# The similarity projection from a row-scaled triangle of M: 64 products for each pair instead of 72, in another order of lists

## The chip, the core and the metric

The kernel runs on one core of a Trainium2 chip. The metric is the device time of one launch in microseconds (us); lower is better.

## The reference, cut to what matters

```python
z_l = h @ W_lang.T ; z_g = h @ W_grav.T ; v = h @ W_V.T      # h: 32 graphs of 256 nodes x 512 features
A_l = max(cosine(z_l, z_l), 0) * not_eye                      # 256 x 256
A_g = exp(-|z_g[n] - z_g[m]|^2 / (2 sigma^2)) * not_eye
K   = w_l * rows_to_one(A_l * adj) + (1 - w_l) * rows_to_one(A_g * adj)
x   = layernorm(x + (K @ v) @ W_O.T)
```

All tensors are float32.

## The kernel before, in words

For each of the two metrics g (L for W_lang, G for W_grav) the kernel forms the symmetric 512 x 512 matrix M = W^T W once. It needs z z^T = h M h^T only in symmetric form, so it computes one matrix X = h^T-side times P, with P = (a part of M) h, and takes X + X^T. Every float32 operand of TensorE is split in two rounded parts (hi and lo, type fp32r): h in `hT_hi`, `hT_lo`; M in `m_hi`, `m_lo`, the halved diagonal blocks in `md_hi`.

**Preparation** (lines 1273 to 1310 on TensorE, `prep_units` at line 282). Units of TensorE work in a fixed list: UPPER (one block row of M's upper triangle), MIRROR (its transposes for the lower blocks), WO_TURN, WVO (the value weights). Four banks of PSUM are used in turn, so a unit waits for the rest part of the fourth unit before it (`prep_lo`, line 1278). ScalarE writes the hi part (line 627; line 628 the halved diagonal block), VectorE the rest (lines 874, 876) and the MIRROR copies (line 869). GpSimd meanwhile splits W_V (lines 516 and 518) and clears the diagonal of the adjacency matrix (lines 524, 527).

**Pairs of graphs.** The 32 graphs are worked through in 16 pairs. TensorE's list of a pair p (line 1413) has, in this order: eight projections (`project`, banks in turn, each waiting until VectorE has finished the one four before it, `proj_ready`, line 1318), the value product 0, four tiles of X (`x_tile`; the first waits for all eight projections, line 1347), value product 1, K times V of graph 0 of the pair before (`k_times_v`), value products 2 and 3, K times V of graph 1. It is a program of 176 matmuls of 512 columns, 72 of them projections:

```python
for i in range(DT):
    steps.append((m_hi[:, g, i, c], lo[i]))
    if i <= j:
        steps.append((m_hi[:, g, i, c] if i < j else md_hi[:, g, i], hi[i]))
        steps.append((m_lo[:, g, i, c], hi[i]))
```

so that the projections of feature block j = 0, 1, 2, 3 have 6, 8, 10 and 12 products, for both g in turn.

Each engine has its own written list of a pair. ScalarE (line 721) rounds each projection (`proj_hi_part`, line 662), saves X, subtracts its diagonal (`centre`), takes exp, scales, rounds K and does the layer norm. VectorE (line 1055) makes the rest parts (`proj_lo_part`, line 921), reads diagonals (line 932), turns blocks (lines 844, 957, 1034), masks and sums, combines K (line 1025), makes its rest part (line 1041) and adds the residual (line 1051). GpSimd (line 572) computes powers of short vectors. SP's list (line 434) holds all transfers of a pair, X and K being spilled to HBM and read back turned. One pair's chain from X to K times V is spread over two passes of these lists: q = p - 1 is the pair before. Passes 0 and 1 and the last two are written out, the rest is a loop of two pairs. The last pair has lists of its own (lines 787, 1189, 1437), which the change leaves as they are.

Of the kernel before, what the change touches and what calls it, by code (L numbers as in the profile page):

```python
# [31 lines left out]
EPS = 1e-8  # L32
LN_EPS = 1e-5
P = 128
# [3 lines left out]
def gnn_resnorm(nc, x, adj, w_lang, w_grav, w_v, w_o, gate_logit, log_sigma, out):  # L38
# [14 lines left out]
    with ExitStack() as ctx:  # L53
# [52 lines left out]
        rden = sb("rden", [P, 2, 2, NT])  # L106
# [15 lines left out]
        scal = sb("scal", [P, 8])  # L122
        last_coef = sb("last_coef", [P, 2, 2, NT])
        last_mean = sb("last_mean", [P, 2, NT])
        last_rstd = sb("last_rstd", [P, 2, NT])
        last_shift = sb("last_shift", [P, 2, NT])

# [85 lines left out]
        adj_ready = sem("adj_ready")  # L213
        scal_exp = sem("scal_exp")
# [82 lines left out]
        def prepared(kind, g, i):  # L297

            return prep_units.index((kind, g, i)) + 1

# [53 lines left out]
        def _(sp):  # L354
# [79 lines left out]
            def pair(p):  # L434

                q = p - 1
                return_x(q, 1)
                spread_r(q, 1)
                load_blocks(p + 1, 1)
                load_x(q, 0)  # L440
                load_x(q, 1)
                spill_k(q, 0)
                load_blocks(p + 2, 0)
                return_k(q, 0)
                spill_k(q, 1)
                store(q - 1, 0)
                store(q - 1, 1)
                spill_x(p, 0)
                store_r(p, 0)
                return_k(q, 1)  # L450
                spread_r(p, 0)
                return_x(p, 0)
                spill_x(p, 1)
                store_r(p, 1)
# [45 lines left out]
        def _(pool):  # L500
# [8 lines left out]

            for k in range(DT):  # L510
                pool.wait_ge(w_loaded[L][k], 16)
# [9 lines left out]

            pool.wait_ge(adj_loaded, 16)
            for t in range(NT):
# [4 lines left out]
                                  r_row[:].rearrange("p t (k a) -> p k t a", a=BLK)).then_inc(adj_ready, 1)  # L528

# [73 lines left out]
        def _(act):  # L603
# [15 lines left out]
            def prep_hi_part(u):  # L619
# [29 lines left out]
            def proj_hi_part(p, k):  # L649
# [6 lines left out]
                if k < 2 * DT:  # L656
                    dst = p_hi[:, :, k // 2, k % 2, :]
                    src = src[:].rearrange("p (b n) -> p b n", b=2)
                else:
                    b, t = divmod(k - 2 * DT, NT)  # L660
                    dst, src = last_v(m_hi, b, t) if is_last(p) else v_hi[:, b, t], src[:]
                nc.scalar.copy(dst, src).then_inc(proj_hi, 1)  # L662
# [58 lines left out]
            def pair(p, parity):  # L721

                q = p - 1
                proj_hi_part(p, 0)
                proj_hi_part(p, 1)
                squares(q - 1, 0)
                proj_hi_part(p, 2)
                proj_hi_part(p, 3)
                proj_hi_part(p, 4)
                gauss_scaled(q, 0)  # L730
                squares(q - 1, 1)
# [4 lines left out]
                normalise(q - 1, 0)  # L736
                gauss_scaled(q, 1)
                save_x(p, 0, 0)
                save_x(p, 0, 1)
                normalise(q - 1, 1)  # L740
                centre(p, 0)
                kt_hi_part(q, 0)
                save_x(p, 1, 0)
                save_x(p, 1, 1)
                turn_hi(p + 1, 1 - parity, 1)
                proj_hi_part(p, 8)
                proj_hi_part(p, 9)
                centre(p, 1)
                kt_hi_part(q, 1)
                proj_hi_part(p, 10)  # L750
                proj_hi_part(p, 11)
                turn_hi(p + 2, parity, 0)
                gauss(p, 0)

            turn_hi(1, 1, 0)
            pair(0, 0)
# [79 lines left out]
        def _(dve):  # L836
# [25 lines left out]
            def prep_lo_part(u):  # L862
# [9 lines left out]
                if kind == UPPER:  # L872
                    if e < D:
                        nc.vector.tensor_tensor(m_lo[:, g, i, e:], src[:, e:], m_hi[:, g, i, e:].bitcast(F32),
                                                ALU.subtract)
                    nc.vector.scalar_tensor_tensor(out=m_lo[:, g, i, a:e], in0=src[:, a:e], scalar=0.5,
# [10 lines left out]
            for u in range(PREP):  # L887
# [4 lines left out]
                if u in SPLIT_AT:  # L892
                    turn_lo(0, 0, SPLIT_AT[u])
# [591 lines left out]
```

## Time and profile before

| | us |
|---|---|
| median of 3 runs (lowest to highest) | 686.14 (685.93 to 686.62) |
| the profiled execution, its own time | 686.16 |
| its span, first to last instruction | 684.4 |
| busy: TensorE, VectorE, ScalarE, GpSimd | 675.4, 518.0, 364.7, 132.4 |

The profile is of one execution. Busy times overlap between engines; a span on GpSimd is rough, and a matmul's drawn duration is longer than its distance to the next, since matmuls are pipelined. What counts on TensorE is the distance between starts. PEld is the load of the stationary operand, which runs beside the matmuls. "Idle before, releaser" tells what an engine waited for.

### The profile page before, as it was taken

The page shows a single profiled execution, that of the slowest core. Times are in us where ns is not written, and L with a number is a line of the kernel's source. Part 1 is how long each engine was busy: PE and PEld are TensorE (multiplying, and loading weights), DVE is VectorE, ACT ScalarE, POOL GpSimd, SP SyncE. Part 2 cuts the span into 40 slices and gives each one's busy share as a digit, 9 for nine tenths or more (in the row PEclk, how much of TensorE's full clock was granted, in tenths as well). Part 3 has the DMA queues.
Part 4 walks back from the last instruction along what each step waited for, and adds up shares of the span by engine and source line. Part 5 has one row for each costly group of instructions (what it writes and reads, how often), then busy time and mean ns, then how long its engine had stood idle before and what let it go on. Part 6 is the DMA issues. An engine that isn't in the chain of part 4 may idle for free.

```text
span 684.4 us, 10995 instructions
## 1 busy us (share of the span) xinstructions
PE 675.4 (99%) x3020; PEld 559.6 (82%) x3020; DVE 518.0 (76%) x1396; ACT 364.7 (53%) x705; POOL 132.4 (19%) x278
## 2 busy tenths in 40 slices
PE   8999999999999999999999999999999999999995
PEld 7888888888888888888888888888888888888884
DVE  4645878788697878869787886978788697877876
ACT  5434445645455564545556454555645455564646
POOL 3302021111222111122211112221111222121122
PEclk9999999999999999999999999999999999999999
DMA  9312726473664647366464636646473664636523
GB/s 291 92 34 67 218 79 191 127 209 112 194 184 141 189 132 197 115 197 181 140 188 131 202 112 196 182 140 188 136 196 112 194 184 141 186 109 184 162 70 123
DMA packets 141510, 106.50 MB, mean 156 GB/s; under 512 B 40112, under 2 KB 115632, under 8 KB 141488
## 3 DMA queue, kind: packets, MB, share of 16 engines
q1 hardware_dynamic: 140768, 104.40, 51.2%
q0 software_dynamic: 288, 1.05, 0.5%
q10 hardware_dynamic: 432, 0.79, 0.3%
q8 instruction: 10, 0.16, 0.1%
q14 instruction: 12, 0.10, 0.0%
HBM read 65.80 MB, written 40.40 MB: 155 GB/s over the span
## 4 chain that ended last, share of the span: by engine, by line
PE 98%; DMA 0%; DVE 0%; issue 0%; ACT 0%; POOL 0%; POOLq 0%
PE bank L1264 95%; PE bank L1286 2%; DMA xs<-in_L_gnn_W_lang 0%; PE bank L1368 0%; PE bank L1296 0%; PE bank L1291 0%; PE bank L1378 0%; DVE xq L1166 0%; DVE p_lo L858 0%; ACT p_hi L617 0%; POOL last_rstd L589 0%; POOLq L53 0%; DVE xq L1186 0%; DVE last_shift L1181 0%; DVE last_rstd L1175 0%
## 5 line engine op out<-in xcount | busy, mean ns | idle before, releaser
L1264 PE MATMUL bank<-hT_lo,m_hi 128*128 128x512 f32 x512 | 168.0, 389 | 0.0
L662 ACT CAST p_hi<-bank 128x512 fp32r<-128x512 f32 x128 | 73.5, 588 | 101.4 <-PE bank L1264 101.4
L1264 PE MATMUL bank<-hT_hi,m_lo 128*128 128x512 f32 x320 | 124.5, 389 | 0.0
L921 DVE TENSOR_TENSOR p_lo<-bank,p_hi 128x512 fp32r<-128x512 f32 x128 | 85.3, 687 | 39.1 <-ACT p_hi L662 37.5
L1264 PEld LDWEIGHTS bank<-hT_lo,m_hi 128*128 128x128 f32 x512 | 96.1, 188 | 20.1 <-DVE p_lo L921 0.2
L662 ACT CAST v_hi<-bank 128x512 fp32r<-128x512 f32 x60 | 32.5, 590 | 132.1 <-PE bank L1264 132.1
L1264 PE MATMUL bank<-wvo_hi,hT_hi 128*128 128x512 f32 x256 | 99.8, 390 | 0.0
L1264 PE MATMUL bank<-wvo_hi,hT_lo 128*128 128x512 f32 x256 | 99.6, 389 | 0.0
L1264 PE MATMUL bank<-wvo_lo,hT_hi 128*128 128x512 f32 x256 | 99.6, 389 | 0.0
L1264 PE MATMUL bank<-p_lo,hT_hi 128*128 128x512 f32 x256 | 99.6, 389 | 0.0
L1264 PE MATMUL bank<-p_hi,hT_hi 128*128 128x512 f32 x256 | 99.6, 389 | 0.0
L537 POOL TENSOR_TENSOR rnorm<-norm,minus_half 128x2 f32<-128x2 f32 x32 | 35.3, 1103 | 256.0 <-DVE norm L938 256.0
L1264 PE MATMUL bank<-hT_hi,m_hi 128*128 128x512 f32 x192 | 74.7, 389 | 0.0
L1264 PEld LDWEIGHTS bank<-hT_hi,m_lo 128*128 128x128 f32 x320 | 60.1, 188 | 12.6
L1051 DVE SCALAR_TENSOR_TENSOR y<-bank,x_nat 128x512 f32<-128x512 f32 x60 | 39.7, 678 | 36.1 <-PE bank L1264 36.1
L932 DVE CUSTOM_DVE_ANT_0 junk_d<-xs,ident 128x128 f32<-128x128 f32 x128 | 29.6, 287 | 38.6 <-ACT xs L673 38.6
L673 ACT COPY xs<-bank 128x512 f32<-128x512 f32 x64 | 36.1, 585 | 38.0 <-PE bank L1264 37.9
L1264 PEld LDWEIGHTS bank<-wvo_hi,hT_hi 128*128 128x128 f32 x256 | 48.1, 188 | 10.0
L1264 PEld LDWEIGHTS bank<-p_hi,hT_hi 128*128 128x128 f32 x256 | 48.1, 188 | 10.0
L1264 PEld LDWEIGHTS bank<-wvo_lo,hT_hi 128*128 128x128 f32 x256 | 48.1, 188 | 9.9
L1264 PEld LDWEIGHTS bank<-p_lo,hT_hi 128*128 128x128 f32 x256 | 48.0, 188 | 10.0
L1264 PEld LDWEIGHTS bank<-wvo_hi,hT_lo 128*128 128x128 f32 x256 | 48.0, 187 | 10.0
(140 smaller groups left out, 1213.4 us busy)
## 6 DMA issues: line engine op xcount, KB each, us to landing
x_blk<-in_x SPq DMA_DIRECT2D x128, 128.0 KB, 3.0
x_spill<-xs SPq DMA_DIRECT2D x30, 512.0 KB, 3.4
xq<-x_spill SPq DMA_DIRECT2D x120, 128.0 KB, 3.1
x_nat<-in_x SPq DMA_DIRECT2D x30, 512.0 KB, 4.7
out_y<-y SPq DMA_DIRECT2D x30, 512.0 KB, 3.0
k_spill<-work SPq DMA_DIRECT2D x30, 256.0 KB, 2.1
work<-k_spill SPq DMA_DIRECT2D x120, 64.0 KB, 2.1
r_row<-r_spill SPq DMA_DIRECT2D x32, 128.0 KB, 3.5
```

The source lines that it names most:

```text
L537: nc.gpsimd.tensor_tensor(rnorm[:, b, 0:NT], norm2[:, b], minus_half[:], ALU.pow).then_inc(pool_steps, 1)
L662: nc.scalar.copy(dst, src).then_inc(proj_hi, 1)
L673: nc.scalar.copy(dst, src).then_inc(x_saved, 1)
L921: nc.vector.tensor_tensor(dst, src, hi.bitcast(F32), ALU.subtract).then_inc(proj_ready, 1)
L932: ins = nc.vector.tensor_tensor_reduce(out=junk_d[:, g, t].rearrange("p (j a) -> p j a", a=BLK), in0=block, in1=ident[:].rearrange("p (j a ...
L1051: nc.vector.scalar_tensor_tensor(out=y[:, b, t], in0=kv_bank[t][:], scalar=1.0, in1=x_nat[:, b, t], op0=ALU.mult, op1=ALU.add, accum_out=r ...
L1264: last = pe.matmul(dst, lhsT, rhs, start=(n == 0), stop=(n == len(steps) - 1))
L1286: last = pe.matmul(dst[:, cols], lhsT, rhs, start=(n == 0), stop=(n == len(steps) - 1))
```

## The change

For a symmetric M any matrix T with T + T^T = M serves on the hi part of h. Before, T was the upper triangle, in hi and rest parts. Now T has, below the diagonal, the hi entries of M alone, and above it the rests; the row of T that belongs to output feature d is scaled by s(d), a number close to 1 with which the rounded diagonal entry becomes exact, and the rests (`m_lo`) are corrected for it. Each block of T is then one rounded operand: `m_lo` for i < j, the joined block `md_hi` for i = j, `m_hi` for i > j. With the four products of `hT_lo` that makes 8 products for every projection, 64 in all.

What else it touches: the scale s is applied where the projection leaves PSUM (ScalarE by an activation with a scale of one number per partition, VectorE by a scalar_tensor_tensor); the four L projections come first, then the four G (`of_projection`); the first projection of a pair waits for the hi parts of h alone and for the rests after four products. In the preparation VectorE reads the diagonals (`diagonals`), computes s (`scales`) and corrects the rests (`scaled_rest`), GpSimd makes two masks and joins the diagonal blocks (`join_triangles`), ScalarE no longer writes a halved block and VectorE has one rest operation for a unit instead of two. The lists of a pair on VectorE, ScalarE and SP are written in another order; `rden` is dropped for `den`.

```diff
@@ GpSimd
+            def join_triangles(g):
+                pool.wait_ge(m_scaled[g], DT)
...
+                for part, (tile, mask) in enumerate(((m_hi, lower_half), (m_lo, upper_strict))):
+                    many, one = diagonal_blocks(tile, g)
+                    nc.gpsimd.tensor_tensor(triangle(part)[:, 0:DT - 1], many.bitcast(F32),
+                                            mask.unsqueeze(1).broadcast_to([P, DT - 1, P]), ALU.mult).then_inc(m_parts[g], 1)
+                    nc.gpsimd.tensor_tensor(triangle(part)[:, DT - 1], one.bitcast(F32), mask, ALU.mult).then_inc(m_parts[g], 1)
+                pool.wait_ge(m_parts[g], 4)
+                nc.gpsimd.tensor_tensor(md_hi[:, g], triangle(0), triangle(1), ALU.add).then_inc(m_ready[g], 1)
@@ ScalarE
-                    nc.scalar.copy(m_hi[:, g, i, i * P:], src[:, i * P:])
-                    nc.scalar.mul(md_hi[:, g, i], src[:, i * P:(i + 1) * P], 0.5).then_inc(prep_hi, 1)
+                    nc.scalar.copy(m_hi[:, g, i, i * P:], src[:, i * P:]).then_inc(prep_hi, 1)
...
+                    nc.scalar.activation(p_hi[:, :, j, g, :], src[:].rearrange("p (b n) -> p b n", b=2), ACT.Copy,
+                                         scale=m_scale[:, g, j:j + 1]).then_inc(proj_hi, 1)
@@ VectorE, preparation
+            def diagonals(g, i):
+                dve.wait_ge(prep_lo, prepared(UPPER, g, i))
+                for s, (tile, sign) in enumerate(((m_hi, 1.0), (m_lo, -1.0))):
+                    nc.vector.tensor_tensor_reduce(
+                        out=x_nat[:, g, s, a:e], in0=tile[:, g, i, a:e].bitcast(F32), in1=ident[:], scale=sign, scalar=0.0,
+                        op0=ALU.mult, op1=ALU.add, accum_out=steps_of[g][:, s, i:i + 1]).then_inc(m_scale_steps[g], 1)
+            def scaled_rest(g):
+                for i in range(DT):
+                    nc.vector.scalar_tensor_tensor(
+                        out=m_lo[:, g, i, i * P:], in0=m_hi[:, g, i, i * P:].bitcast(F32), scalar=steps_of[g][:, 4, i:i + 1],
+                        in1=m_lo[:, g, i, i * P:].bitcast(F32), op0=ALU.mult, op1=ALU.add).then_inc(m_scaled[g], 1)
...
+                if kind == UPPER and g == L:
+                    diagonals(L, i)
+                    if i == DT - 1:
+                        scales(L)
+                        scaled_rest(L)
+                if kind == UPPER and g == G and i < DT - 1:
+                    diagonals(G, i)
...
+                if (kind, g, i) == (MIRROR, G, 1):
+                    diagonals(G, DT - 1)
+                    scales(G)
+                if (kind, g, i) == (WVO, None, 1):
+                    scaled_rest(G)
@@ VectorE, a pair: the order now (lo k is proj_lo_part)
+ gram(q,0,L) gauss_masked(q,0) lo0 cosine_masked(q,0) row_factors(q,0) lo1 lo2 turn_x(q,1) lo3
+ kernel_sum(q,0) gram(q,1,G) lo4 inverse_masked(q,1) gram(q,1,L) lo5 lo6 lo7 gauss_masked(q,1)
+ cosine_masked(q,1) row_factors(q,1) turn_lo(p+1,0) kernel_sum(q,1) diagonal(p,0) turn_k(q,0)
+ turn(p+1,1) turn_r(p,0) kt_lo(q,0) diagonal(p,1) turn_lo(p+1,1) residual(q,0,0) turn(p+2,0) lo8
+ turn_r(p,1) turn_k(q,1) lo9 kt_lo(q,1) residual(q,0,1) turn_x(p,0) gram(p,0,G) residual(q,1,0)
+ residual(q,1,1) lo10 inverse_masked(p,0) lo11
@@ SP, a pair: the order now
+ load_blocks(p+1,1) load_blocks(p+2,0) return_x(q,1) spread_r(q,1) spill_k(q,0) return_k(q,0)
+ store(q-1,0) spill_k(q,1) load_x(q,0) spill_x(p,0) return_k(q,1) store_r(p,0) return_x(p,0)
+ spill_x(p,1) store(q-1,1) load_x(q,1) spread_r(p,0) store_r(p,1)
@@ TensorE
                 for i in range(DT):
+                    stationary = m_lo[:, g, i, c] if i < j else md_hi[:, g, i] if i == j else m_hi[:, g, i, c]
+                    pe.matmul(pbank(k)[:], stationary, hi[i], start=(i == 0), stop=False)
+                if k == 0:
+                    pe.wait_ge(hT_ready, upto(p, 2, 2))
+                for i in range(DT):
+                    last = pe.matmul(pbank(k)[:], m_hi[:, g, i, c], lo[i], start=False, stop=(i == DT - 1))
```

In the first pair TensorE waits for `m_ready[L]` before projection 0 and for `m_ready[G]` before projection 4; VectorE waits for both before its first list.

## Rows read from the trace of the kernel before

**Rows 1.** The page, busy time of each engine and TensorE's granted clock in tenths

```profile
PE 675.4 (99%) x3020; PEld 559.6 (82%) x3020; DVE 518.0 (76%) x1396; ACT 364.7 (53%) x705; POOL 132.4 (19%) x278
...
PEclk9999999999999999999999999999999999999999
```

**Rows 2.** The chain that ended last: start us, us, what

```profile
30.39 624.78 PE bank L1264 x2756
```

**Rows 3.** One pair, its projections: us, then busy (x) of PE, PEld, DVE, ACT, POOL

```profile
349.40:389.30 39.90, 39.90 (x178) 33.03 (x176) 31.41 (x85) 21.86 (x42) 7.74 (x16) 1.00 0.53 165
349.40:365.70 16.30, 16.30 (x73) 13.51 (x72) 14.72 (x37) 9.96 (x21) 3.61 (x9) 1.00 0.61 176
```

**Rows 4.** Groups: out<-in, shapes xcount | busy us, mean ns | idle before

```profile
L1264 PE MATMUL bank<-hT_lo,m_hi 128*128 128x512 f32 x512 | 168.0, 389 | 0.0
...
L1264 PE MATMUL bank<-hT_hi,m_lo 128*128 128x512 f32 x320 | 124.5, 389 | 0.0
...
L1264 PE MATMUL bank<-hT_hi,m_hi 128*128 128x512 f32 x192 | 74.7, 389 | 0.0
```

**Rows 5.** Groups: emptying a projection, and the nearest rows to its new forms

```profile
L662 ACT CAST p_hi<-bank 128x512 fp32r<-128x512 f32 x128 | 73.5, 588 | 101.4 <-PE bank L1264 101.4
...
L921 DVE TENSOR_TENSOR p_lo<-bank,p_hi 128x512 fp32r<-128x512 f32 x128 | 85.3, 687 | 39.1 <-ACT p_hi L662 37.5
...
L1051 DVE SCALAR_TENSOR_TENSOR y<-bank,x_nat 128x512 f32<-128x512 f32 x60 | 39.7, 678 | 36.1 <-PE bank L1264 36.1
...
L685 ACT ACTIVATE work<-work,scal 128x512 f32<-128x512 f32 x25 | 18.2, 730 | 0.0
```

**Rows 6.** Timeline of that pair: start us, us, what, idle before and its releaser

```profile
348.24 0.69 DVE L1051 SCALAR_TENSOR_TENSOR y<-bank,x_nat 128x512 f32<-128x512 f32 x1 [2.49 <-PE bank L1264]
...
376.39 0.65 DVE L1041 TENSOR_TENSOR kt_lo<-work,kt_hi 128x512 fp32r<-128x512 f32 x1
...
378.42 0.39 PE L1264 MATMUL bank<-v_hi,kt_hi 128*128 128x512 f32 x1
```

**Rows 7.** Transfers by line: KB each, median us from issue to landing

```profile
xq<-x_spill SPq DMA_DIRECT2D x120, 128.0 KB, 3.1
x_nat<-in_x SPq DMA_DIRECT2D x30, 512.0 KB, 4.7
```

**Rows 8.** Timeline of the last pair: TensorE and VectorE

```profile
628.66 0.39 PE L1264 MATMUL bank<-hT_lo,m_hi 128*128 128x512 f32 x1
...
631.87 0.68 DVE L921 TENSOR_TENSOR p_lo<-bank,p_hi 128x512 fp32r<-128x512 f32 x1
...
646.61 0.69 DVE L921 TENSOR_TENSOR p_lo<-bank,p_hi 128x512 fp32r<-128x512 f32 x1
...
647.75 0.39 PE L1264 MATMUL bank<-p_hi,hT_hi 128*128 128x512 f32 x1
```

**Rows 9.** Timeline of the preparation: GpSimd, VectorE, TensorE

```profile
14.12 0.61 POOL L516 CAST v_hi<-xq 128x512 fp32r<-128x512 f32 x1 [6.24 <-DMA xq<-in_L_gnn_W_V]
14.81 1.29 POOL L518 TENSOR_TENSOR v_lo<-xq,v_hi 128x512 fp32r<-128x512 f32 x1
...
17.28 0.56 DVE L874 TENSOR_TENSOR m_lo<-bank,m_hi 128x384 fp32r<-128x384 f32 x1 [2.85 <-ACT md_hi L628]
...
18.92 0.38 PE L1291 MATMUL bank<-ident,m_hi 128*128 128x128 f32 x2
...
35.70 0.39 PE L1264 MATMUL bank<-hT_lo,m_hi 128*128 128x512 f32 x1
```

**Rows 10.** GpSimd and VectorE side by side in one pair, and a group

```profile
334.32 0.69 POOL L537 TENSOR_TENSOR rnorm<-norm,minus_half 128x2 f32<-128x2 f32 x1 [11.03 <-DVE norm L938]
...
338.04 1.23 DVE L852 TENSOR_TENSOR hT_lo<-hT_raw,hT_hi 128x1024 fp32r<-128x1024 f32 x1
338.27 1.54 POOL L537 TENSOR_TENSOR rnorm<-norm,minus_half 128x2 f32<-128x2 f32 x1 [2.34 <-DVE norm L938]
...
L932 DVE CUSTOM_DVE_ANT_0 junk_d<-xs,ident 128x128 f32<-128x128 f32 x128 | 29.6, 287 | 38.6 <-ACT xs L673 38.6
```

More of the change, by code:

```diff
@@ L32 @@
 EPS = 1e-8
+TINY = 1e-35
 LN_EPS = 1e-5
@@ L122, in gnn_resnorm @@
         scal = sb("scal", [P, 8])
+        m_scale = sb("m_scale", [P, 2, DT])
         last_coef = sb("last_coef", [P, 2, 2, NT])
@@ L126, in gnn_resnorm, with diagonal_blocks, split_blocks, triangle @@
         last_shift = sb("last_shift", [P, 2, NT])
+        lower_half = junk_d[:, 0, 0]
+        upper_strict = junk_d[:, 0, 1]
+        steps_of = [junk_d[:, 1, 1, 32 * g:32 * g + 32].rearrange("p (s j) -> p s j", j=DT) for g in range(2)]
+        def diagonal_blocks(tile, g):
+            flat = tile[:, g].rearrange("p k d -> p (k d)")
+            step = D + P
+            return (flat[:, 0:(DT - 1) * step].rearrange("p (i w) -> p i w", w=step)[:, :, 0:P], flat[:, (DT - 1) * step:])
+        def split_blocks(tile, g):
+            flat = tile[:, g].rearrange("p k c -> p (k c)")
+            return (flat[:, 0:(DT - 1) * P].rearrange("p (i c) -> p i c", c=P), flat[:, (DT - 1) * P:])
+        def triangle(part):
+            return junk_a[:].rearrange("p t (k c) -> p t k c", c=P)[:, part]
         COS, GAUSS, KER = range(3)
@@ L213, in gnn_resnorm @@
         adj_ready = sem("adj_ready")
+        masks_cleared = sem("masks_cleared")
+        masks_ready = sem("masks_ready")
+        m_scale_steps = [sem(f"m_scale_steps{g}") for g in range(2)]
+        m_scaled = [sem(f"m_scaled{g}") for g in range(2)]
+        m_parts = [sem(f"m_parts{g}") for g in range(2)]
+        m_ready = [sem(f"m_ready{g}") for g in range(2)]
         scal_exp = sem("scal_exp")
@@ L299, in prepared, with of_projection @@
             return prep_units.index((kind, g, i)) + 1
+        def of_projection(k):
+            return k % DT, k // DT
         def upto_unit(u):
@@ L1081, in pair @@
                 turn_k(q, 0)
+                turn(p + 1, 1)
                 turn_r(p, 0)
-                turn(p + 1, 1)
                 kt_lo_part(q, 0)
@@ L1086, in pair @@
                 turn_lo(p + 1, 1 - parity, 1)
+                residual(q, 0, 0)
+                turn(p + 2, 0)
+                proj_lo_part(p, 8)
                 turn_r(p, 1)
-                turn(p + 2, 0)
-                residual(q, 0, 0)
-                residual(q, 0, 1)
-                proj_lo_part(p, 8)
                 turn_k(q, 1)
@@ L1312, in project @@
             def project(p, parity, k):
-                j, g = divmod(k, 2)
+                j, g = of_projection(k)
                 if k == 0:
-                    pe.wait_ge(hT_ready, upto(p, 2, 2))
+                    pe.wait_ge(hT_hi_ready, upto(p, 2, 2))
+                if type(p) is int and p == 0 and j == 0:
+                    pe.wait_ge(m_ready[g], 1)
+                    pe.wait_ge(prep_lo, prepared(MIRROR, g, DT - 1))
                 if not (type(p) is int and p == 0 and k < 4):
```

129 lines of the change are left out of this document (76 added, 53 removed).

## The prediction, made blind

> **What bounds the kernel now.** The page comes first: TensorE is busy for 675.4 of 684.4 us at the full granted clock, 2.4 GHz, and no other engine is over 76% [rows 1]. Busy time alone doesn't make a bound, so the chain of waits is next: one unbroken piece of 624.78 us holds 2,756 products of line 1264 [rows 2], 0.2267 us from start to start. A pair is 176 of them, 39.9 us, which is what the stage table shows for one pair, with VectorE busy for 31.4 us and ScalarE for 21.9 [rows 3]. So every product taken out of a pair gives back 0.2267 us, as long as the other engines' lists keep up. They have less room than their averages tell: within the projections VectorE is busy for 14.7 of 16.3 us [rows 3].
>
> **Products removed.** The projections are 72 a pair: 512, 320 and 192 in the three groups [rows 4], and 128 with the halved diagonal blocks, 1,152 over 16 pairs. Afterwards 64 x 16 = 1,024. 128 x 0.2267 = **-29.0 us**. A pair becomes 168 x 0.2267 = 38.1 us.
>
> **Emptying a projection.** VectorE's subtraction, 687 ns, becomes a scalar_tensor_tensor from PSUM; the residual, 678 ns, has that form [rows 5]. I take no change. ScalarE's cast, 588 ns, becomes an activation with a scale for each partition. Bounds: 0 to +0.14 us, by the 730 ns of the nearest activation over 512 columns [rows 5]; I take the upper end, 1.1 us a pair on an engine with 16 us to spare, and 0.14 us later for VectorE.
>
> **The order within a pair.** I laid the new lists beside TensorE's, from T, the start of a pair: projection k ends at 1.81(k+1), the value product at 17.2, the X tiles at 19.1 to 24.5, K times V of graph 0 runs from 27.2 and that of graph 1 from 35.4 to 38.1. A result reaches ScalarE 0.2 us later. Durations are those of before (a rest part 0.60 us from start to start). VectorE's pass ends with the residual that the last product releases, then lo10, the masked inverse and lo11: free at T+2.7. After the L sum and the masked exp it makes lo0 by T+4.6; projection 4 wants it at T+7.3. With the cosine, the factors and the turn between, lo3 is ready at T+9.0 (wanted at 12.7), lo4 at T+11.6 behind ScalarE's scaling and layer norm (wanted at 14.5), lo7 at T+16.1 (wanted by the first X tile at 17.2). X must be saved at T+21.7 for the fourth tile at 22.7. K's rest part of graph 0 is ready at T+25.7 for 27.2, a margin of 1.5 us; before, it ended at 377.04 for 378.42, 1.4 us [rows 6]. On SP the load of x for graph 1, once issued early in a pair, now stands behind the second store: issued at T+32.3, landing 4.7 us later at T+37.0 [rows 7], just when the residual of graph 1 wants it at 36.9; some tenths there are covered, since VectorE waited 2.49 us for TensorE ahead of that residual [rows 6]. The return of X of graph 1 goes behind eight block loads (3.7 us of issues): issued by T'+2.4 of the next pair, landing 3.1 us later [rows 7] at T'+5.5, wanted at T'+7.1. Every margin is at least 1.0 us, so the steady pairs cost **0**. If VectorE's cover of lo7 (1.1 us) were gone, each 0.1 us beyond it would cost 1.4 us over the 14 pairs.
>
> **The last pair** keeps its lists, made for projections of 6 to 12 products. There VectorE works without a pause from lo0 at 631.87 to lo7, ended at 647.30, 18.64 us after the first projection at 628.66; the X tile wanted it at 647.75 [rows 8], 19.09 after. The wish moves to 17.2. The chain starts 0.4 us sooner, so lo7 comes at 18.2: **+1.0 us** (between 0.5 and 2).
>
> **The preparation.** Removed: eight halved blocks on ScalarE (0.17 us each) and eight small rest operations on VectorE (some 0.15 us each, merged). Added on VectorE for each g: eight diagonal readings of 0.22 us from start to start (287 ns each [rows 10]), four tiny steps of 0.2, four corrections of 0.6, 0.47, 0.34 and 0.2: 4.2 us. For L they fit mostly into VectorE's idle time of 2.85 us before the rest part at 17.28 [rows 9]: without anything else the cost is 0.4 us, where the rests of WO_TURN come 0.3 us late. For G, the joins on GpSimd are 384, 128, 384, 128 and 512 columns at the 1.29 us for 512 of its two-input row [rows 9]: 4.1 us. The correction of G ends near 36.2, the join at 40.4; projection 4 of the first pair wants it at 35.70 [rows 9] + 7.3 = 43.0. Covered, with 2.6 us to spare, and VectorE's wait for it covered too.
>
> But the L part falls into the time in which GpSimd works without a gap on W_V, 14.12 to 21.8 [rows 9]. The trace shows that the two engines get in each other's way: a GpSimd operation of 0.69 us took 1.54 when it met VectorE's two-input subtraction that had begun at 338.04, and ended 0.54 us after it [rows 10]. The other direction no row shows. Bounds: 0.4 us if VectorE never waits. If it waits for a GpSimd operation at each of its instructions with two SBUF inputs, two diagonal readings, one small step and the four corrections alternate with the eight operations on W_V; the correction ends at 22.3, not 17.3, the rest of the first G unit at 22.9, and TensorE's MIRROR at 18.92 starts at 23.0: 4.1 us late. The G diagonals against the L join then add up to 4: 8 in all. I take **+5 us**, all of the L part and one more, since the row shows the handover within such meetings, and the G part has idle time before it. The Trainium skill (SBUF — State Buffer, "Who interferes with whom") states both directions: a VectorE instruction with two SBUF inputs and a GpSimd one that reads SBUF exclude each other for a whole instruction. By that rule the term is nearer its upper end; the trace agrees as far as rows 10 go.
>
> Sum: 686.16 - 29.0 + 1.0 + 5.0 = 663.2 us; the profiled execution is 0.02 us above the median.
>
> **Rivals.**
> (a) VectorE does not wait for GpSimd: the preparation costs 0.4 us, 658.6 us. For it: no row shows the wait. Against it: the opposite wait is plain [rows 10].
> (b) A steady wait: one of the margins of 1.0 to 1.6 us is gone, say by 0.3 to 0.8 us in each pair, because lo7, X's copy or K's rest part is later than my tally; 14 x 0.3 to 0.8 = 4 to 11 us on top of either case, 665 to 675. For it: VectorE's list is nearly full in the projections [rows 3]. Against: its busy time in a pair is 31.4 of 38.1 us, and nothing big is added.
> (c) Slower than before: SP, which works strictly in order, becomes the pace. Its return of X of graph 0 now follows the return of K and the store of norms; from there the chain goes over the turned X, exp and the masked exp to lo0, with 4.7 us of slack at the masked exp and 2.7 at lo0. If it came over 7.4 us late in each pair, each pair would wait, and from 7.4 + 1.8 us the gain would be gone; at 10 us late, 686.2 - 29.0 + 16 x 2.6 = 699 us. For it: the waits for centred X, for K and for the layer norm now stand in one row ahead of it. Against: its issues are 22 us of 38.
> That the change doesn't do what it says is excluded by its loops: eight products a projection are written out.
>
> **The numbers.** Forecast 0.5; (a) 0.3; (b) 0.17; (c) 0.03. Predicted 663.2 us. The range reaches down to (a) with all 29.0 us kept, 657.5, and up to 8 us of preparation and a little of (b), 669. About 0.2% can be told from no change here. Faster 0.96, within it 0.01, slower 0.03.
>
> **What the profile would show.** 64 projection products a pair and 168 x 0.2267 = 38.1 us from one pair's start to the next; no waits of TensorE in the loop (b would show them ahead of an X tile or of K times V); a gap of about 1 us before the first X tile of the last pair; in the preparation diagonal readings and corrections on VectorE stretched or late beside the splits of W_V, a MIRROR that starts near 23 and the first projection near 41 instead of 35.7. Were this at 36, (a) holds; a pair longer than 38.3 us would make the forecast wrong in its main part.

## The result, and the profile after

| | before | after |
|---|---|---|
| median of 4 runs each, us (lowest to highest) | 686.03 (685.80 to 686.62) | 666.14 (664.92 to 666.75) |
| profiled execution, its span | 686.16, 684.4 | 666.75, 665.0 |
| mean granted clock of TensorE in it | 0.998 | 0.993 |

The ratio of the runs is 0.9706, 95% interval 0.969 to 0.9723: 19.9 us faster. The forecast of 663.2 us was 2.9 us too low, inside its range of 657.5 to 669.0. The span shrank by 19.4 us, where the sum of the prediction had 23.0.

The page of the changed kernel: busy time of each engine, the granted clock, and the groups that answer to [rows 1, 4, 5]. In it and below, line 1435 has the products of a projection with `hT_hi`, 1439 those with `hT_lo`, 1370 the other products of the pairs, X tiles among them, and those of WVO, 1397 the MIRROR transposes, 718 ScalarE's and 1016 VectorE's part of emptying a projection; where an experiment adds or removes lines, these numbers shift by up to three.

```profile
PE 650.5 (98%) x2892; PEld 538.4 (81%) x2892; DVE 538.7 (81%) x1438; ACT 376.6 (57%) x697; POOL 138.8 (21%) x292
...
PEclk9799999999999999999999999999999999999999
...
L1439 PE MATMUL bank<-hT_lo,m_hi 128*128 128x512 f32 x512 | 136.8, 389 | 0.0
L718 ACT ACTIVATE p_hi<-bank,m_scale 128x512 fp32r<-128x512 f32 x128 | 87.6, 686 | 74.3 <-PE bank L1439 73.3
...
L1016 DVE SCALAR_TENSOR_TENSOR p_lo<-bank,m_scale,p_hi 128x512 fp32r<-128x512 f32 x128 | 92.7, 742 | 17.8 <-ACT p_hi L718 17.5
```

3,020 matmuls have become 2,892: the 128 are gone. ScalarE's scaled cast takes 686 ns where the plain one took 588; VectorE's scaled rest takes 742 where the subtraction took 687. The second digit of the clock row is a 7 where before there were only nines.

The chain of waits of the changed kernel, two neighbouring pairs, and the stage table of one pair (columns as in [rows 3]):

```profile
91.08 23.57 PE bank L1370 x104
...
129.16 23.57 PE bank L1370 x104
```

```profile
349.40:387.48 38.08, 38.08 (x170) 31.53 (x169) 31.47 (x85) 22.67 (x42) 7.38 (x16) 1.00 0.61 171
```

A pair's 104 other products start 38.08 us after those of the pair before, 168 x 0.2267, and TensorE has no idle time in between. The first projection of the last pair starts at 609.53, that of the first pair at 43.77: 565.76 us for 15 pairs, where before it was 628.66 - 35.70 = 592.96. The difference, 27.20 us, is 15 x 8 x 0.2267. So the steady part is as forecast, to 0.01 us; what is left is ahead of it and behind it.

**Ahead: the preparation.** The timeline of the changed kernel, VectorE, GpSimd and TensorE (compare [rows 9]; line 947 reads a diagonal, 957 is the first tiny step of the scales, 968 corrects the rests, 560 is the second operation of a split of W_V):

```profile
14.81 1.06 DVE L947 CUSTOM_DVE_ANT_0 x_nat<-m_hi,ident 128x128 f32<-128x128 f32 x1
...
16.41 1.28 POOL L560 TENSOR_TENSOR v_lo<-xq,v_hi 128x512 fp32r<-128x512 f32 x1
16.52 1.20 DVE L957 TENSOR_SCALAR junk_d<-junk_d 128x4 f32<-128x4 f32 x1
...
18.38 4.33 DVE L968 SCALAR_TENSOR_TENSOR m_lo<-m_hi,junk_d,m_lo 128x512 fp32r<-128x512 f32 x4
...
23.36 0.44 PE L1397 MATMUL bank<-ident,m_hi 128*128 128x128 f32 x2 [3.92 <-DVE m_lo L935]
...
42.47 1.93 DVE L968 SCALAR_TENSOR_TENSOR m_lo<-m_hi,junk_d,m_lo 128x512 fp32r<-128x512 f32 x4
```

A diagonal reading takes 0.29 us alone and 1.06 beside a split. A step on 4 elements, begun 0.11 us after the split at 16.41, ends at 17.72, 0.03 us after the split does. The four corrections take 4.33 us beside the splits and 1.93 at 42.47, where GpSimd is idle. MIRROR, at 18.92 before, starts at 23.36: 4.44 us late. The same stretch as a table of stages (span, then busy of PE, PEld, DVE, ACT, POOL, then the granted clock):

```profile
22.00:24.00 2.00, 0.44 (x2) 0.20 (x2) 1.97 (x6) 0.00 (x0) 1.38 (x3) 0.96 0.00 0
24.00:26.00 2.00, 1.34 (x7) 1.35 (x8) 1.97 (x8) 0.19 (x1) 1.92 (x4) 0.50 0.04 8
26.00:28.00 2.00, 2.00 (x11) 2.00 (x11) 2.00 (x4) 0.39 (x1) 1.94 (x4) 0.50 0.01 4
28.00:30.00 2.00, 2.00 (x11) 2.00 (x11) 1.41 (x7) 0.51 (x2) 0.56 (x1) 0.50 0.00 0
30.00:32.00 2.00, 2.00 (x17) 1.98 (x15) 1.57 (x3) 1.03 (x2) 0.00 (x0) 0.83 0.00 0
```

After TensorE's idle 3.9 us its granted clock fell to 0.50, the 1.2 GHz level, some 0.2 us before the end of the first row, and stayed there until some 0.7 us into the last row (0.7 x 0.5 + 1.3 over 2 us gives the 0.83), some 6.8 us in all, although TensorE was busy again. The first projection came 8.07 us late: 4.44 for MIRROR, 0.9 for one more wait (the copy of line 931), and 2.7 that are left for the half clock. The preparation is the least steady part of the kernel: experiments 4, 5, 6, 7 and 11 leave it as it is, and in their traces the first projection starts at 43.81, 43.77, 43.18, 42.31 and 43.05. Over the six the delay is 6.6 to 8.1 us, and the traced execution lies at its upper end; a difference of up to 1.5 us between the first projections of two single traces can be there without any edit to the preparation.

**Behind: the last pair.** Its first projection and first X tile, and VectorE's first and last rest part between them, after:

```profile
609.53 0.39 PE L1435 MATMUL bank<-hT_hi,md_hi 128*128 128x512 f32 x1
...
612.40 0.74 DVE L1016 SCALAR_TENSOR_TENSOR p_lo<-bank,m_scale,p_hi 128x512 fp32r<-128x512 f32 x1
...
627.51 0.75 DVE L1016 SCALAR_TENSOR_TENSOR p_lo<-bank,m_scale,p_hi 128x512 fp32r<-128x512 f32 x1
...
628.32 0.50 PE L1370 MATMUL bank<-p_hi,hT_hi 128*128 128x512 f32 x1 [0.57 <-DVE p_lo L1016]
```

18.79 us from the first projection to the X tile, where 76 products need 17.23: 1.56 lost, and 0.30 less than the 19.09 before (84 products, 19.04, so that 0.05 was lost there). VectorE's chain from the start of lo0 to the end of lo7, without a pause in both kernels, takes 15.86 us; before it took 15.43 [rows 8]. From the X tile to the end it is 36.68 us (36.65 before). Together: -27.20 + 8.07 - 0.30 + 0.03 = -19.4 us, the whole difference of the spans.

### The profile page after: what moved, and what is told of

It is laid out like the page before. It is cut to its first block, busy times and chain, and to the rows that moved or that the text cites. A ratio compares the mean times of both kernels' runs of the same rounds, so it can differ in the third digit from the quotient of the medians.

```text
span 665.0 us, 10795 instructions
## 1 busy us (share of the span) xinstructions
PE 650.5 (98%) x2892; PEld 538.4 (81%) x2892; DVE 538.7 (81%) x1438; ACT 376.6 (57%) x697; POOL 138.8 (21%) x292
## 4 chain that ended last, share of the span: by engine, by line
PE 92%; DVE 4%; DMA 1%; ACT 1%; issue 0%; SPq 0%; POOL 0%; POOLq 0%; DVEq 0%; ACTq 0%
PE bank L1370 57%; PE bank L1435 16%; PE bank L1439 16%; PE bank L1392 1%; DMA x_nat<-in_x 1%; DVE m_lo L968 1%; DVE x_nat L947 1%; DMA xs<-in_L_gnn_W_lang 0%; PE bank L1402 0%; DVE p_lo L1016 0%; DVE work L1071 0%; PE bank L1478 0%; DVE m_lo L935 0%; DVE work L1105 0%; ACT y L778 0%
## 5 line engine op out<-in xcount | busy, mean ns | idle before, releaser
L1439 PE MATMUL bank<-hT_lo,m_hi 128*128 128x512 f32 x512 | 136.8, 389 | 0.0
L718 ACT ACTIVATE p_hi<-bank,m_scale 128x512 fp32r<-128x512 f32 x128 | 87.6, 686 | 74.3 <-PE bank L1439 73.3
L1016 DVE SCALAR_TENSOR_TENSOR p_lo<-bank,m_scale,p_hi 128x512 fp32r<-128x512 f32 x128 | 92.7, 742 | 17.8 <-ACT p_hi L718 17.5
L722 ACT CAST v_hi<-bank 128x512 fp32r<-128x512 f32 x60 | 34.9, 581 | 118.7 <-PE bank L1370 118.6
L1435 PE MATMUL bank<-hT_hi,m_lo 128*128 128x512 f32 x192 | 59.2, 390 | 0.3 <-DVE p_lo L1016 0.3
L1435 PE MATMUL bank<-hT_hi,m_hi 128*128 128x512 f32 x192 | 59.1, 389 | 0.0
L1435 PE MATMUL bank<-hT_hi,md_hi 128*128 128x512 f32 x128 | 49.8, 389 | 0.0
L623 POOL TENSOR_TENSOR msq<-row_sq,one_by_d 128x2 f32<-128x2 f32 x30 | 5.9, 198 | 197.8 <-ACT junk_a L770 197.7
```

The costliest lines, as they stand in the source:

```text
L718: nc.scalar.activation(p_hi[:, :, j, g, :], src[:].rearrange("p (b n) -> p b n", b=2), ACT.Copy, scale=m_scale[:, g, j:j + 1]).then_inc(pr ...
L722: nc.scalar.copy(last_v(m_hi, b, t) if is_last(p) else v_hi[:, b, t], src[:]).then_inc(proj_hi, 1)
L1016: nc.vector.scalar_tensor_tensor(out=p_lo[:, :, j, g, :], in0=src[:].rearrange("p (b n) -> p b n", b=2), scalar=m_scale[:, g, j:j + 1], in ...
L1435: pe.matmul(pbank(k)[:], stationary, hi[i], start=(i == 0), stop=False)
L1439: last = pe.matmul(pbank(k)[:], m_hi[:, g, i, c], lo[i], start=False, stop=(i == DT - 1))
```

## The experiments

The theory after the result: the steady pairs and the price of a product are as forecast; the 8 us are one cause and its follower, VectorE held by GpSimd's work on W_V, and TensorE's clock after the idle time that this makes. All runs change the changed kernel. "First projection" and "last pair" are the starts of the first projections of the first and the last pair in the profiled execution. The kernel before was timed again beside them: 686.75 us beside experiments 1, 2, 3 and 5, 685.98 beside 4, 6, 7 and 8, 685.86 beside 9, 10 and 11; each ratio is to that time. Where one execution is all there is (experiments 1, 3, 4, 5, 11), its time has no interval.

**1. GpSimd starts on W_V later.**

```diff
             for h in range(2):
                 load_w(pool, 2, w_v, h)
+            pool.wait_ge(m_scaled[L], DT)
             for k in range(DT):
```

> The changed kernel with one wait more: GpSimd starts to split W_V only when the L rests are corrected. VectorE's list is untouched. Theory (exclusion): VectorE's L part, ended at 22.6 us now, ends at 17.5 to 18, the wait at the MIRROR of block row 2 is gone; the splits end near 25.5, so the first WVO product waits for them, 1 to 3 us late; first projection at 37 to 40 us. Rival (VectorE's own work is the delay): the L part ends no sooner than 22 us and the first projection, with the splits delayed as well, starts later than 43.8.

One execution: 660.85 us, span 659.1, 5.9 under the changed kernel's. VectorE at the corrections, GpSimd at its first split, and VectorE's first step of the scales of G, in this run:

```profile
15.64 1.93 DVE L969 SCALAR_TENSOR_TENSOR m_lo<-m_hi,junk_d,m_lo 128x512 fp32r<-128x512 f32 x4
...
17.49 0.69 DVE L936 TENSOR_TENSOR m_lo<-bank,m_hi 128x512 fp32r<-128x512 f32 x1
...
17.65 0.61 POOL L559 CAST v_hi<-xq 128x512 fp32r<-128x512 f32 x1 [9.66 <-DVE m_lo L969]
...
28.68 1.20 DVE L958 TENSOR_SCALAR junk_d<-junk_d 128x4 f32<-128x4 f32 x1
```

The same instructions on the same data take 1.93 us, not 4.33, and all that has changed is that GpSimd is idle beside them. The wait of 3.9 us is gone, the clock was 1.00 in every stretch from 18 to 38, and the first projection came at 37.97 instead of 43.77. So an added wait makes the kernel faster; what VectorE does for L stayed in its place, so its own length is not what made these 5.8 us. The splits, now later, meet VectorE's work for G instead: a reading of G took 1.36 us beside a split, and the step on 4 elements shown last took 1.20 beside a join.

**2. VectorE's last reading, scales and corrections of L later**, behind the first rest part of WVO:

```diff
-                    diagonals(L, i)
-                    if i == DT - 1:
-                        scales(L)
-                        scaled_rest(L)
+                    if i < DT - 1:
+                        diagonals(L, i)
+                if (kind, g, i) == (WVO, None, 0):
+                    diagonals(L, DT - 1)
+                    scales(L)
+                    scaled_rest(L)
```

> The changed kernel, but VectorE reads the last L diagonal, computes the L scales and corrects the L rests only after the rest part of the first WVO unit, when GpSimd has long finished splitting W_V. Theory (the two engines exclude each other on operations that read SBUF, and TensorE then loses its clock too): no TensorE wait of 3.9 us at the MIRROR of block row 2, the four corrections take 1.9 us instead of 4.3, the first projection starts at 36 to 38 us instead of 43.8, and the time is 659 to 661 us. Rival (VectorE's added 4.2 us of work, wherever it stands, is what delays TensorE): the delay comes later in the preparation but stays, first projection at 41 us or later, 664 us or more.

663.0 us (662.59 to 663.42, two executions; ratio 0.9647, 0.9606 to 0.9688), 2 us above what I had written. First projection at 38.00, no idle 3.9 us and the clock at 0.999: the same answer from VectorE's side. But a part of the cost moved, as the waits of TensorE show:

```profile
PE bank L1437 <- DVE m_hi L931: 1.8, 1, 1.8
...
PE bank L1437 <- POOL md_hi L578: 0.8, 1, 0.8
```

The late corrections make the join of L late (0.8 us) and the copies of MIRROR that the first projections' banks wait for (1.8). The last pair starts 568.07 us after the first projection, not 565.76.

**3. TensorE kept busy through the wait.**

```diff
             for u in range(PREP):
+                if u == prepared(MIRROR, L, 2) - 1:
+                    for n in range(18):
+                        pe.matmul(kv_bank[1][:], kt_hi[:, 0, 0, 0], in_kt(kt_hi, 0), start=True, stop=True)
                 prepare(u)
```

> The changed kernel with 18 products of 512 columns of zeros into a free bank (about 4.1 us) ahead of the MIRROR unit that waits 3.9 us. Nothing else changes: VectorE's L part still ends at 22.6 us. Theory (of the 8.1 us by which the first projection starts later, 4.8 are waits and 3.3 the granted clock of 0.5 from 24 to 30.5 us that follows them): the clock stays at 1.0, TensorE still waits for VectorE until 23.4, the first projection starts at 40 to 41 us, the time falls by 3 us. Rival (all 8.1 us are waits for VectorE, the low clock covers nothing more): first projection at 43 us or later.

One execution: 664.92 us, span 663.2, no less than the lowest of the changed kernel's four, so the time alone shows nothing; the trace has to. Here the collision stays (the four corrections took 4.73 us) and only the fall of the clock is taken away; the stages of this run:

```profile
20.00:24.00 4.00, 3.37 (x16) 2.53 (x14) 3.96 (x6) 0.00 (x0) 3.92 (x4) 1.00 0.03 7
24.00:31.00 7.00, 5.63 (x43) 5.21 (x44) 6.93 (x21) 2.31 (x5) 4.86 (x8) 1.00 0.00 1
```

MIRROR started at 22.98 (23.36 in the changed kernel), the first projection at 41.90 (43.77). From MIRROR to the first projection it is 18.92 us, where the changed kernel has 20.41 and the five other traces with its preparation 19.9 to 21.1. So the half clock costs some 1.5 us that nothing else takes over (1.0 to 2.2 against the other traces); less than the 3 us I had expected, because at full clock TensorE next waits for VectorE (1.2 us at the MIRROR copies, 0.8 at `hT_lo`, in place of 0.9).

**4. L and G projections in turn again.**

```diff
-            return k % DT, k // DT
+            return k // 2, k % 2
```

> The changed kernel with L and G projections in turn as in the kernel before, instead of four L and then four G. The joined G block, ready at 48.7 us, is then wanted by the second projection at 45.6 instead of the fifth at 51.0. Theory: TensorE waits for it once, 2.5 to 3.5 us, in the first pair, and pairs stay at 38.08 us; 669 to 670 us. Rival (order within the projections does not matter, or matters in every pair since the G sums come first on VectorE): 666.8 us, or pairs over 38.2 us.

One execution: 669.94 us, as I had written, 3.2 us above the changed kernel's profiled run. TensorE, and what it waited for, in this run:

```profile
PE bank L1435 <- POOL md_hi L578: 2.9, 1, 2.9
```

GpSimd's join of G ended at 48.66. With L first, projection 4 needs it 7.3 us after projection 0; in turn, projection 1 does, after 1.8. This shows that the joins of G are covered in the changed kernel, and by what: there the join ended at 48.68 and projection 4 started at 51.03, 2.35 us to spare.

**5. The old order of the lists within a pair**, on VectorE, ScalarE and SP. The core of the edit on SP:

```diff
-                load_blocks(p + 1, 1)
-                load_blocks(p + 2, 0)
...
+                load_blocks(p + 1, 1)
+                load_x(q, 0)
+                load_x(q, 1)
...
-                store(q - 1, 1)
-                load_x(q, 1)
-                spread_r(p, 0)
```

> The changed kernel with the lists of a pair of VectorE, ScalarE and SP in the order of the kernel before; products, preparation and TensorE's list as changed. Theory (the old order was made for projections of 6 to 12 products; in it VectorE works through the q sums, masks and the turn ahead of lo6 and lo7, and the masked exp of graph 1 behind lo7): a pair gets longer than 38.1 us by 0.3 to 1.5 us, 671 to 687 us in all, with TensorE waiting for VectorE's p_lo ahead of the first X tile. Rival (the reordering gives nothing, the products alone give the gain): 38.1 us a pair, 665 to 668 us.

One execution: 667.47 us, span 665.5, within 0.5 of the changed kernel's. First projection 43.77, last pair 609.53, to the hundredth as with the new lists: the new order brings nothing to the steady pairs, and my theory that the old one would cost something in each pair was wrong. Only the last pair's X tile came 0.35 us later than in the changed kernel, 19.14 us after its first projection. The new order has one visible trace, a load that comes late. The line of the residual in the changed kernel, and in experiment 6:

**6. The load of x for graph 1 behind that of graph 0.**

```diff
                 load_x(q, 0)
+                load_x(q, 1)
                 spill_x(p, 0)
...
                 store(q - 1, 1)
-                load_x(q, 1)
```

> The changed kernel, but SP issues the load of x for graph 1 right behind that for graph 0 instead of behind the second store. Theory (the wait of VectorE's residual for that load, 1.6 to 1.7 us in each pair, is covered in the steady pairs but starts VectorE's unbroken chain in the last pair late): pairs stay at 38.08 us, the residual no longer waits for the load, the first X tile of the last pair comes 17.7 to 18.1 us after its first projection instead of 18.8, the time falls by 0.7 to 1.1 us. Rival (the last pair loses 1.5 us to its lists alone): no change, within 0.3 us.

```profile
609.37 0.69 DVE L1154 SCALAR_TENSOR_TENSOR y<-bank,x_nat 128x512 f32<-128x512 f32 x1 [1.74 <-DMA x_nat<-in_x]
```

```profile
607.78 0.69 DVE L1154 SCALAR_TENSOR_TENSOR y<-bank,x_nat 128x512 f32<-128x512 f32 x1 [0.73 <-PE bank L1370]
...
609.14 0.69 DVE L1154 SCALAR_TENSOR_TENSOR y<-bank,x_nat 128x512 f32<-128x512 f32 x1 [0.66 <-PE bank L1370]
```

The first fence is the changed kernel, the second this run: the wait for the transfer is gone. The time is 666.27 us (665.31 to 666.8; ratio 0.971, 0.9694 to 0.9727), the same as without the edit, so my theory was wrong and the rival right. In place of the one wait for the transfer VectorE now has two for TensorE, 0.73 and 0.66 us, and its lo0 starts 2.74 us after the last pair's first projection instead of 2.87. The X tile comes 18.67 us after it instead of 18.79, where I had expected 17.7 to 18.1.

**7. The last pair's list fitted to 8 products.** The rest parts of VectorE come sooner, the masked sums and the turn of K later, and ScalarE rounds projection 7 ahead of the first layer norm:

```diff
             proj_hi_part(p, 6)
+            proj_hi_part(p, 7)
             normalise(q - 1, 0)
-            proj_hi_part(p, 7)
...
-            cosine_masked(q, 1)
             proj_lo_part(p, 3)
+            cosine_masked(q, 1)
+            proj_lo_part(p, 4)
...
-            kernel_sum(q, 1)
             proj_lo_part(p, 5)
             proj_lo_part(p, 6)
-            turn_k(q, 0)
             proj_lo_part(p, 7)
+            kernel_sum(q, 1)
+            turn_k(q, 0)
```

> The changed kernel with the last pair's lists fitted to projections of 8 products: VectorE makes rest part 3 ahead of the cosine mask, 4 ahead of the exp mask, and 5 to 7 ahead of the sum of K of graph 1; ScalarE scales projection 7 ahead of the first layer norm. Theory (the last pair's 1.5 us are VectorE's queue ahead of the rest parts): the first X tile comes 17.3 to 18.0 us after the first projection instead of 18.8 and the end moves with it, 0.8 to 1.5 us less. Rival (the chain behind the X tiles, K of graph 1 by SP's spill and return, then sets the end): the X tile comes sooner and the time stays.

668.46 us (667.97 to 669.06; ratio 0.9746, 0.973 to 0.9763): 2.3 us slower. The rival that I had written down came true, and more than that, since it had the time stay. The X tile did come sooner, 18.18 us after the first projection instead of 18.79. But K of graph 1 was spilled later, and its return holds ScalarE's list, in this run:

```profile
633.64 0.71 DVE L1137 STREAM_TRANSPOSE work<-work 128x512 f32<-128x512 f32 x1 [3.78 <-DMA work<-k_spill]
...
634.44 0.62 ACT L761 CAST kt_hi<-work 128x512 fp32r<-128x512 f32 x1 [3.64 <-DVE work L1137]
...
636.77 0.66 PE L1478 MATMUL bank<-ident,xs 128*128 128x128 f32 x4 [2.53 <-ACT xs L739]
```

Behind that cast in ScalarE's order stands the centring of X, behind that turn in VectorE's order the reading of X's diagonal, and TensorE waited 2.53 us for the centred X. The lost 1.56 us in the last pair can't be had by this reordering; whether by another I did not try.

**8. The preparation spread on VectorE's side**: scales of L and two diagonals of G behind MIRROR of G, block row 1, corrections of L behind the first WVO rest part, the last diagonal and the scales of G behind the second, corrections of G behind the last MIRROR.

```diff
-                    if i == DT - 1:
-                        scales(L)
-                        scaled_rest(L)
...
+                if (kind, g, i) == (WVO, None, 0):
+                    scaled_rest(L)
...
                 if (kind, g, i) == (MIRROR, G, 1):
+                    scales(L)
+                    diagonals(G, 0)
+                    diagonals(G, 1)
+                if (kind, g, i) == (WVO, None, 1):
                     diagonals(G, DT - 1)
                     scales(G)
-                if (kind, g, i) == (WVO, None, 1):
+                if (kind, g, i) == (MIRROR, G, DT - 1):
                     scaled_rest(G)
```

> The changed kernel with the preparation's VectorE work spread over its idle times behind GpSimd's splits of W_V: L scales and the first two G diagonals after the first G MIRROR copy, the corrections of L after the first WVO rest part, the last G diagonal and the G scales after the second, the corrections of G after the last MIRROR copy. Only the fourth L diagonal still meets the splits. Theory (exclusion): no wait over 1 us of TensorE in the preparation, full clock throughout, first projection at 36 to 37 us, the join of G done by 42.5 us and not waited for; 658.5 to 660.5 us in all. Rival (VectorE's added work is the cost): first projection at 40 us or later, or as long a wait for the join of G at the fifth projection.

662.6 us (662.3 to 663.09; ratio 0.966, 0.9644 to 0.9676), 2 us above what I expected. The first projection came at 35.60, 0.1 us before that of the kernel before: with the work at these places nothing is left of the 8.07 us. This run changes both what meets and where VectorE's work stands, so by itself it does not tell the two apart; experiments 1 and 10, which leave VectorE's work for L in its place, do. And the work has to be somewhere. In this run

```profile
45.27 2.73 DVE L1019 SCALAR_TENSOR_TENSOR p_lo<-bank,m_scale,p_hi 128x512 fp32r<-128x512 f32 x4 [1.38 <-POOL md_hi L578]
```

VectorE's first list waits for the join of G, which ended at 45.04. In its first pair TensorE waited 1.2 us for a MIRROR copy, 0.3 for a rest part of WVO and 0.8 for one of a projection. The last pair starts 569.16 us after the first projection: 3.4 of the 8.2 us were given back in the first pair.

**9. The added wait of experiment 1 again, five executions.** The kernel is that of experiment 1.

> The one added wait again (GpSimd starts on W_V only once VectorE has corrected the rests of L), now in five rounds, because the look at it gave 660.85 us. Theory (the preparation's loss is a meeting of VectorE and GpSimd): 660.5 to 661.5 us as median, 5 us under the changed kernel. Rival (the look was a lucky execution, the difference is noise of the run): above 663 us.

661.4 us (661.06 to 662.37), ratio 0.9645 (0.9632 to 0.9659). The interval lies wholly under that of the changed kernel (0.969 to 0.9723): 4.2 us better by the ratios and 4.7 by the medians, for one line. In its trace the first projection starts at 38.28.

**10. The rest of the meetings taken apart**, on top of that wait:

```diff
-            join_triangles(L)
             pool.wait_ge(adj_loaded, 16)
...
+            pool.wait_ge(m_scale_steps[G], 2 * DT + 4)
+            join_triangles(L)
             join_triangles(G)
...
-                if kind == UPPER and g == G and i < DT - 1:
-                    diagonals(G, i)
...
-                    diagonals(G, DT - 1)
+                    for n in range(DT):
+                        diagonals(G, n)
                     scales(G)
```

> On top of that wait, the rest of the meetings is taken apart: all eight diagonal readings of G come together behind MIRROR of G, block row 1, when GpSimd has finished W_V, and GpSimd joins the diagonal blocks of L only after VectorE's scales of G. Theory (each meeting costs what it shows, and nothing else is lost in the preparation): no reading longer than 0.3 us, the tiny first step of the scales 0.17 instead of 1.20, TensorE's waits of 0.9 and 0.9 us between 19 and 27 us gone or under 0.5 together, first projection at 36.0 to 36.8 instead of 37.97; the join of L is done by 35.5 and does not delay it. Time 658.8 to 660.0. Rival (the second unit of delay is VectorE's own added work, or the join of L at its new place comes late): first projection at 37.5 or later, 660.5 us or more.

661.29 us (660.2 to 661.91; ratio 0.9643, 0.9629 to 0.9656). The timeline of this run, TensorE, VectorE and TensorE:

```profile
25.54 0.47 PE L1371 MATMUL bank<-hT_hi,v_hi 128*128 128x512 f32 x1 [1.56 <-POOL v_lo L561]
...
28.18 0.17 DVE L959 TENSOR_SCALAR junk_d<-junk_d 128x4 f32<-128x4 f32 x1
...
37.16 0.39 PE L1436 MATMUL bank<-hT_hi,md_hi 128*128 128x512 f32 x1
```

The tiny step of G, 1.20 us beside a join in experiments 1 and 9, is at 0.17, and all but two of the readings are at 0.3 (0.48 and 0.74 beside GpSimd's work on the adjacency matrix). TensorE's waits for VectorE between 19 and 27 us are gone. One wait is left, 1.56 us for the rest part of W_V, whose last operation GpSimd now ends at 25.44, 3.3 us later than in the changed kernel. The first projection is at 37.16, above the 36.0 to 36.8 I had written, and 37.16 - 35.70 = 1.46: this one wait is the whole delay, and it is one for GpSimd: with the meetings gone, TensorE waits for VectorE nowhere in the preparation. In the trace the span is 1.2 us under that of experiment 9; the medians differ by 0.1, and 661.29 us is what I had written for the rival, not for the theory (658.8 to 660.0). So the times do not show that this part is worth anything.

**11. A ninth product in every projection.** The first of the four products with `hT_lo` is done twice; that part of the result then counts once too often.

```diff
-                for i in range(DT):
+                for i in (0, *range(DT)):
                     last = pe.matmul(pbank(k)[:], m_hi[:, g, i, c], lo[i], start=False, stop=(i == DT - 1))
```

> The changed kernel with a ninth product in each projection (the first of the four with the rest part of h is done twice, so the low part counts once too often): 128 products more. The term of the products by itself, the other way. Theory (TensorE's stream sets the pace, nothing else is near it): 128 x 0.2267 = +29.0 us in pairs of 39.9, less what the last pair hides (about 1 us, as its lists then have their slack again): 694 to 695.5 us. Rival (the 64-product pair was already partly held by another engine): under 693 us, since the longer pair would give that engine its slack back.

One execution: 693.4 us, span 691.6, +26.6 to the changed kernel's. That is between the two numbers I had put down, 694 for the theory and 693 for its rival; the starts decide it. One pair and the last pair's first X tile:

```profile
350.00:389.90 39.90, 39.90 (x178) 33.04 (x177) 31.99 (x85) 22.72 (x43) 7.71 (x16) 1.00 0.59 165
```

```profile
655.05 0.41 PE L1370 MATMUL bank<-p_hi,hT_hi 128*128 128x512 f32 x1
```

From the first projection (43.05) to the last pair (636.01) it is 592.96 us, as in the kernel before. The X tile comes 19.04 after the last pair's first projection, (72 + 12) x 0.2267, without a wait: the same lists that lose 1.56 us at 64 products lose nothing at 72. The sum is +27.20, +0.25 in the last pair, -0.72 in the preparation, 26.7 for the 26.6 of the span. The theory of the stream holds; my number was off because the last pair hides 1.56 us of the 1.81, where I had put 1, and because the preparation, in which nothing was changed, happened to be 0.7 us shorter in this execution.

## Why the prediction was right, and where it was off

- **Products removed, -29.0 us, and steady pairs 0.** Shown. 27.20 of it in 15 pairs, both ways (experiment 11), the rest in the last pair. Rival (b), a steady wait, did not occur: TensorE has no wait from the first projection of the first pair to that of the last. Rival (c) neither; SP's order makes one residual of a pair wait for x (1.74 us in the line shown), and taking this away changes nothing (experiment 6). I had written "some tenths there are covered"; it was more than tenths, and covered still.
- **ScalarE +0.14 us** measured +0.10 (588 to 686 ns). **VectorE "no change"** was wrong: 687 to 742 ns, +0.055. The row I took it from, the residual, is the same operation from PSUM, but with the constant 1.0 where this one reads a number per partition. In the steady pairs it is covered.
- **The last pair, +1.0 us** (0.5 to 2): 1.56, of which 0.05 was lost before, so 1.5. The step that failed is "the chain starts 0.4 us sooner, so lo7 comes at 18.2": it started 0.34 us sooner (2.87 us after the first projection, before 3.21) and ended at 18.73. For it had also grown, from 15.43 to 15.86 us, by 0.43, and eight rest parts at +0.055 are 0.44. The term that I had put at nothing in the steady pairs, where it costs nothing, came back here.
- **The preparation, +5 us** (0.4 to 8): 8.07. The part of it for L was right in its mechanism and nearly in size: "MIRROR at 18.92 starts at 23.0", measured 23.36 (21.8 to 23.7 in the six traces with this preparation), and experiments 1 and 2 show it from both sides. Rival (a), that VectorE does not wait for GpSimd, is wrong for these operations. By the rule of the Trainium skill that I cited (SBUF — State Buffer, "Who interferes with whom") the term was to be nearer its upper end. Meetings of a whole instruction occurred as it says (the 4.33 us against 1.93), but the waits for VectorE that they made add up to 5.3 us (4.44 and 0.9), close to the 5 that I had taken for the meetings of L and one more; to the upper end it was the clock that brought the term. That page also says that a `tensor_scalar` can hold or wait for the shared ports when it runs in a two-port mode. The trace agrees as far as it goes (in which mode the step ran no row shows): on 4 elements it took 1.20 us beside a split, 0.17 alone. I had counted only instructions with two inputs.
- **What the term left out** is the clock: a wait of 3.9 us did not cost 3.9, but brought 6.8 us at 1.2 GHz behind it. By difference this is 2.7 us, by experiment 3 it is some 1.5. **And what it bounded too high** is the part of G, "up to 4": its joins are covered by the order L first (experiment 4), and its readings and scales, taken out of the meetings, brought the first projection 1.1 us forward (experiment 10 against 9, one trace each) and the median not at all. So it is in part luck that 8.07 lies at the upper bound of 8: the bound was made of meetings of G that cost little, and the measured value of a clock that the bound did not have.

The sum of the span by the prediction's terms: -29.0 + 1.0 + 5.0 = -23.0. Measured: -29.0 + 1.5 + 8.1 = -19.4. The 2.9 us by which the forecast was too low are thus 3.1 of the preparation and 0.5 of the last pair, less the 0.6 by which the median lies under the traced execution (666.14 against 666.75), all within 0.1.

The version that beats both kernels is the changed one with one added wait: 661.4 us, 0.9645 of the kernel before.

## What to carry to other kernels

In a stream bound by TensorE, count products in the steady part and believe the count; spend the doubt on the two ends, where the lists were fitted to the old length. When VectorE gets new work beside a long run of GpSimd work, count each meeting at up to the length of GpSimd's instruction, small operations too, and see first whether GpSimd's work has slack: letting it start later gained more here (4.7 us) than moving VectorE's work about. And price an idle stretch of TensorE with the half clock that may follow it; here that was some 1.5 us behind a wait of 3.9.

## What the runs showed of the hardware that I had not expected

- An instruction of VectorE on 128x4 elements, one input, was held until a GpSimd instruction ended: 1.20 us against 0.17, in the changed kernel beside a split and in experiments 1 and 9 beside a join. The four corrections took 4.33 us against 1.93.
- After 3.9 us without work TensorE ran at half clock for some 6.8 us, most of them busy, and in experiment 11 through three rows of 2 us after a wait of 2.9, as in experiment 7. With waits of at most 1.8 us (experiments 1, 2, 8, 10) the granted clock of the whole run was 0.997 to 0.999.
- On 512 columns out of PSUM an activation with a scale for each partition took ScalarE 98 ns more than a cast, and a scalar_tensor_tensor with one took VectorE 55 ns more than a subtraction. No run tells the scale from the change of the instruction.
